# Left products of a depthwise convolution on GpSimd instead of VectorE, with a new order of pieces

## The chip, the cores and the metric

The kernel runs on one core of a Trainium2 chip. Its time is the device time of one execution in microseconds (us). Below, PE is TensorE (PEld its weight loads), DVE is VectorE, ACT is ScalarE, POOL is GpSimd and SP is SyncE.

## The reference

The program takes 32 samples of 128 tokens by 256 features, with a context of 128 by 192 each, through four layers. Each layer adds to x the output of a cross-attention and then of a feed-forward block, each times tanh of a gate. The four feed-forward blocks are a quantized pair of linear maps with a convolution between them, a mixture of experts with one expert per token, a small transformer block, and three blocks with dequantized weights. The change touches the first:

```python
h = bit_linear(x, w1)                                  # 256 -> 1024 features, quantized
h = depthwise_conv1d(h.transpose(0, 2, 1), conv_w, conv_b)   # 3 taps over the tokens, per channel
h = h.transpose(0, 2, 1)
h = jax.nn.silu(h)
return bit_linear(h, w2)                               # 1024 -> 256, quantized
```

A convolved value is its channel's left weight times the token before, plus the centre weight times the token itself, plus the right weight times the token after, plus a bias.

## The kernel before

Four lanes (0 to 3) each take one sample at a time, in eight passes, through two sequences of stages. The first is L0 (attention), bit (the block above), L1 (attention with wide heads) and route (the choice of experts); when all eight passes are through it, each lane goes on with mix, L2, self and L3, eight passes again. Eight lanes of a second kind then carry the last feed-forward block (L3f), four passes each. The sequence with the convolution ends near 1260 us; nothing in the second half has a convolution.

Every stage of every lane is written once per engine, as a generator that yields after each piece. An engine has one instruction queue, worked off in order. The order of the lanes' pieces in it is written out by hand or by a planner in the strings `ORDER` (L165): each character is the number of a lane, and `turns` (L331) runs that lane's generator to its next yield. So a piece waits not only for its semaphores but also for everything ahead of it in the string. Semaphores are counted by the names in `STAGE`, one counter for each lane and engine.

The stage bit, per lane and pass. VectorE normalizes and rounds x (L797 to L803); TensorE multiplies by w1 (h0 and h1, 512 columns of each of two PSUM banks). VectorE scales them into `hid`, 128 partitions by 8 channel groups by 128 tokens, in two halves of four groups (L809, signals hid0 and hid1). ScalarE makes the centre tap with the bias into `act_h` (L1288, four instructions for a half, signals cen0 and cen1). VectorE then adds the left products (L817, signal left) and the right products (L821, signal conv) to `act_h`. Each of these is a multiply-add with a weight per partition, so it takes one channel group of 127 tokens at a time, four instructions for a half, and L821 waits for L817's last. ScalarE makes tanh from it (L1295), VectorE the silu (L828), the maximum over the channels (L832) that TensorE transposes (L377), the scale (L836 to L840), the scaled and rounded values (L845, L851), which TensorE multiplies by w2 (L353), and the sum into x (L855).

GpSimd, before the change, does in the first sequence: variance and its power -1/2 for each normalization (`pool_rstd`, L1382 and L1384; VectorE's L711 waits for them), the keys of L0 spread over heads (L1399, two for a sample), bias sums (L1411, L1419), the softmax factors of L1 (L1424, four for a sample; TensorE's transposes L377 wait for them), the weight of the expert (L1442, L1444) and indirect DMAs (L1476, L1485, L1498). In the stage bit it has only `pool_rstd`.

`head_keys` are two buffers of 128 by 512 per lane, used by the attention stages L0 and L1 and free in between, during bit. `hid` and `act_h` are parts of the lane's buffer `big`, and `w["conv"]` holds three weights for each channel side by side. In the profile's names all of these are `big`, `head_keys` and `w_conv`.

Of the kernel before, what the change touches and what calls it, by code (L numbers as in the profile page):

```python
# [15 lines left out]
P = 128  # L16
# [44 lines left out]
        "pool": NORM["pool"],  # L61
# [94 lines left out]
def sequence_a(n):  # L156

    for half in (FIRST, SECOND):
# [8 lines left out]
        "3231314231212111323213121121213234230231023113100222200033331111313121323210301301030101131030200123"  # L167
        "2332131310210232021213212130120313012120323132013130120123121032302011312103302232332023020120122333"
        "3001220221001101312312132100101100210230203110210312300020231212231320130121033012201321302110132123"
        "1210323021011213032020320330232122301320320103313202132032031010023331213010201111200312302032013012"  # L170
        "3131322221002003131231213130323120132012031130231231210231302323131012021023003030223202332321301030"
        "1322022133033101010002121010201313113200120203012310130232120203001213223123131032013203112102303110"
        "2123102131202023031101122002303302321223013203012033132021302320311000233312130012011112003123020320"
        "1301201231232312211223331300202012331231310102202330211302121302210313213102320321102112023020203303"
        "1222100230313031313120301301201303330212010102121200113023012300301021301003201323232121201302310130"
        "2130210210331210120231121321012012013210321131132200230302223212301203023123012230120213310310103330"
        "3033202311321002330233210201101020103203011300220021323232130203210131012212103013023132321132132012"
        "1321210123123203012111032202032030230231313010033022322103303101031033002102110012303313100102012023"
        "0231320100201232312023012103210310130321320211213303210123012031021031232302102131312301220202103213"
        "2310033032112221331201313020323200101121220302123233032012213031013021121323131231321321121323321312"  # L180
        "3021000202113130203201312100101330120310123323030020132311121303223213120103230203211210010331312003"
        "2231213032031122013033323012020121323102123100012122133230023110310310210321032012312130100010230010"
        "2232311312323202300211021033103121203310213203203230212021010130220313202113212030302112131330010103"
        "3203103123223032030110220120112312333010212023120001210221303210130101213312030230032302121230031021"
        "2312001022032011201232011031231021312302320123111022102330310101330322323002301321210031013102302022"
        "3213013021201332301232032320212110003212333003011023103201310233131201303213002032313100322102130032"
        "2021013201202331121303100123120332301322131132103022020121130203203111001030130102321212033210303203"
        "2132001022122031023332103201223203031100123331132313021001013230213300102212130022021012302130233112"
        "1303100213120332301322131132103022020121130203230111313300101033203103123232021010322033323001220233"
        "2130202003310120230132231130230300102321123001012310010220302303122312123012302301123310232312310232"  # L190
        "1213020121203202323010111033130202223032013131202303211011221231023023121303212200102331003010201330"
        "1301322132132010032230211012213201023210213003101302030213221010033130222330113123120312032102302330"
        "3101110331302022230320131312320302101122121021302331312301133212030102133210301302301130102103213212"
        "133012201002083722870020283838702802370830a97879a80330738a979a0793a09738a30937a830a378a9a8b909cb87ca"
        "07b08acb8c8bc90b97ac0a8b78bc89ab789ab7a0c80a9c8b0ba9ca798a79bab8c7007ac8a0b870b87b0c8cb0a9a79769565c"
        "9cb6c5b65b6c59a65b9c7ac675ca675c659756b9ab5c658c96898598b5b966caca56a565ba56cb96cb79cb5c6956a756b9c7"
        "56c8bc97a5bc65b7687a9ca5c56677886c96596565bc5b98a96a56856a8b657b5789a6b956c5b7cb7c8b6ac685a578ac7a6c"
        "765865b659c7959b9b6cb6587a56c865c59ba796b565"
    ),
    "dve": (  # L200
        "1302130424413214213411441213221321323022131131313133132131212232321321301322203103030000100130120020"
        "2101301023013112123233033010232212231210113112102301101313132302032302120101310223323221231213232032"
        "3213201101002002002130103100320101010302102020132230231202112011331321033131121013001213212102012032"
        "0022032322312311203323231323023313013323120020013010132300110100203021200300133202222312331131303102"
        "0111302113120120210231213131032203023300202212311202333232132303331011200220030013132100011010203020"
        "2010030133222221020331103112011331311210130012131212010220302203203232212311203233231323023313013323"
        "1202000001010123311322210030000010202023023230120023133013301201311211012322121101200132212120213202"
        "0311300332031231320123330122333301320130210002033001001201301310302001122300122212200310223113111021"
        "1331311210331020112332112220003212100232002213213213203232302321333330310301200132023300002000331010"
        "1201021323113002221322122313023101101211331031211331302120102312100130222002232100213321302312202333"  # L210
        "3330313021032100233030000200110101003201311322130220102233220132111231330302013323002023201203001213"
        "0313213013112112123202201000200003212231321311331320303313021202312201130110201300033323100032120223"
        "2102131113323310131100020311202123202221232031300133220101311030231323301230212023011002211300231003"
        "3200133201232202131201031100332033011112301120212320122200300122101132230323113032103201032300221033"
        "1122101002310032031320332231221030121031100102113132302323021230212003002202103131130312333023133021"
        "0232021020031101210030323130321202321021013100102130313213103122232012220030012002032031313310121330"
# [1188 lines left out]
def pool_cross(pool, m, t, p, l, src):  # L1405
# [635 lines left out]
```

## Time and profile before

| | us |
|---|---|
| median of 3 runs | 2839.97 |
| lowest and highest | 2837.9, 2842.7 |
| the profiled execution | 2830.95 |
| its span, first to last instruction | 2829.7 |
| TensorE busy | 2597.7 (92%) |
| VectorE busy | 2187.3 (77%) |
| ScalarE busy | 1684.6 (60%) |
| GpSimd busy | 1134.9 (40%) |
| mean granted TensorE clock | 0.975 |

Busy time is a sum over the whole span. What a change to one stage is worth has to be read in that stage, so the views below take the stretch from 70 to 1250 us, in which the setup is over and the convolution's sequence runs, apart from the rest. In a row of the groups, "L817 DVE ... big<-big,w_conv ... x250 | 74.9, 361 | 10.1 <-ACT big L1288 10.0" is: line 817 on VectorE, what it writes and reads, 250 instructions, 74.9 us busy together, 361 ns the mean of one, and 10.1 us in which the engine stood idle before them, 10.0 of them ended by ScalarE's L1288. Instructions of one engine overlap a little, so busy time is less than count times mean.

### The profile page before, as it was taken

The page shows a single profiled execution, that of the slowest core. Times are in us where ns is not written, and L with a number is a line of the kernel's source. Part 1 is how long each engine was busy: PE and PEld are TensorE (multiplying, and loading weights), DVE is VectorE, ACT ScalarE, POOL GpSimd, SP SyncE. Part 2 cuts the span into 40 slices and gives each one's busy share as a digit, 9 for nine tenths or more (in the row PEclk, how much of TensorE's full clock was granted, in tenths as well). Part 3 has the DMA queues.
Part 4 walks back from the last instruction along what each step waited for, and adds up shares of the span by engine and source line. Part 5 has one row for each costly group of instructions (what it writes and reads, how often), then busy time and mean ns, then how long its engine had stood idle before and what let it go on. Part 6 is the DMA issues. An engine that isn't in the chain of part 4 may idle for free.

```text
span 2829.7 us, 60900 instructions
## 1 busy us (share of the span) xinstructions
PE 2597.7 (92%) x23748; PEld 2122.2 (75%) x23748; DVE 2187.3 (77%) x4794; ACT 1684.6 (60%) x4539; POOL 1134.9 (40%) x1981
## 2 busy tenths in 40 slices
PE   7797989899888989999899999999999999999999
PEld 5676767677666767777777777888787878788777
DVE  7868697877678587786767777787878787778998
ACT  4565666666555666666555555655656565656544
POOL 2132323323443543324454444333333333435676
PEclk9898999999899999999999999999999999999999
DMA  6000000000011121100012121100000000000110
GB/s 189 3 24 9 18 13 18 14 13 18 11 48 40 63 77 42 30 16 24 11 46 62 55 76 58 33 19 20 21 16 21 16 24 13 24 3 25 33 36 21
DMA packets 84168, 92.15 MB, mean 33 GB/s; under 512 B 15332, under 2 KB 77288, under 8 KB 83880
## 3 DMA queue, kind: packets, MB, share of 16 engines
q1 hardware_dynamic: 75432, 59.91, 6.9%
q0 software_dynamic: 8448, 28.34, 3.4%
q8 instruction: 188, 3.08, 0.5%
q14 instruction: 100, 0.82, 0.1%
HBM read 65.36 MB, written 22.85 MB: 31 GB/s over the span
## 4 chain that ended last, share of the span: by engine, by line
PE 63%; DVE 23%; ACT 5%; POOL 4%; issue 3%; DMA 1%; SPq 1%; DVEq 0%; POOLq 0%; ACTq 0%
PE psum L353 14%; PE psum L377 12%; PE psum L346 12%; PE psum L403 6%; DVE tiny L730 4%; PE psum L415 3%; PE psum L532 3%; DVE big L738 3%; PE psum L370 3%; PE psum L360 3%; PE psum L367 2%; PE psum L526 2%; PE psum L513 2%; DVE xn L711 1%; DVE tiny L766 1%
## 5 line engine op out<-in xcount | busy, mean ns | idle before, releaser
L377 PE MATMUL psum<-ident,big 128*128 128x128 f32 x2784 | 428.2, 285 | 66.2 <-ACT big L1219 22.4
L377 PEld LDWEIGHTS psum<-ident,big 128*128 128x128 f32 x2784 | 324.0, 145 | 140.2 <-ACT big L1219 49.3
L1219 ACT ACTIVATE big<-big 128x512 f32<-128x512 f32 x512 | 312.1, 631 | 170.4 <-DVE big L738 168.5
L730 DVE TENSOR_REDUCE tiny<-psum 128x8 f32<-128x1024 f32 x256 | 312.3, 1220 | 47.5 <-PE psum L403 42.8
L738 DVE TENSOR_TENSOR big<-psum,tiny 128x512 f32<-128x512 f32 x512 | 329.6, 685 | 8.8
L1382 POOL TENSOR_SCALAR tiny<-mv 128x1 f32<-128x1 f32 x224 | 53.0, 236 | 677.1 <-DVE mv L701 674.9
L403 PE MATMUL psum<-head_keys,small 64*128 64x256 f32 x2048 | 285.9, 403 | 19.7 <-ACT big L1226 10.9
L1399 POOL TENSOR_TENSOR head_keys<-big,head_rows 128x512 f32<-128x512 f32 x256 | 266.6, 1060 | 0.0
L1424 POOL TENSOR_TENSOR big<-big,tiny 128x512 f32<-128x512 f32 x128 | 133.8, 1052 | 308.2 <-DVE tiny L773 308.0
L403 PEld LDWEIGHTS psum<-head_keys,small 64*128 64x128 f32 x2048 | 185.3, 189 | 74.6 <-issue 56.9
L1263 ACT ACTIVATE big<-psum,tiny 128x128 f32<-128x128 f32 x512 | 181.7, 382 | 38.1 <-DVE tiny L768 37.6
L1226 ACT ACTIVATE head_keys<-psum 128x512 f32<-128x512 f32 x256 | 144.4, 599 | 39.9 <-PE psum L377 38.5
L377 PE MATMUL psum<-ident,small 128*128 128x128 f32 x896 | 154.6, 282 | 10.6 <-ACT small L1230 5.7
L711 DVE TENSOR_SCALAR xn<-x,mv,tiny 128x256 f32<-128x256 f32 x192 | 112.7, 588 | 64.9 <-POOL tiny L1384 64.5
L1226 ACT ACTIVATE big<-psum 128x512 f32<-128x512 f32 x256 | 146.0, 597 | 27.5 <-PE psum L377 25.4
L1384 POOL TENSOR_TENSOR tiny<-tiny,minus_half 128x1 f32<-128x1 f32 x224 | 129.1, 576 | 18.6
L377 PEld LDWEIGHTS psum<-ident,small 128*128 128x128 f32 x896 | 102.6, 141 | 43.0 <-issue 12.0
L346 PE MATMUL psum<-xnT,w_L 128*128 128x128 f32 x1024 | 127.3, 278 | 1.7 <-ACT xnT L1250 1.6
L346 PE MATMUL psum<-xnT,w_up 128*128 128x128 f32 x1024 | 126.0, 277 | 0.0
L532 PE MATMUL psum<-w_L,head_keys 128*128 128x256 f32 x512 | 124.7, 387 | 1.2 <-ACT head_keys L1273 1.1
L346 PEld LDWEIGHTS psum<-xnT,w_L 128*128 128x128 f32 x1024 | 120.3, 192 | 7.4 <-issue 3.4
L346 PEld LDWEIGHTS psum<-xnT,w_up 128*128 128x128 f32 x1024 | 119.2, 192 | 3.4 <-issue 2.5
(334 smaller groups left out, 6616.7 us busy)
## 6 DMA issues: line engine op xcount, KB each, us to landing
ctxT<-in_ctxT SPq DMA_DIRECT2D x64, 128.0 KB, 2.2
after_L_xattn<-x SPq DMA_DIRECT2D x64, 128.0 KB, 1.7
mixture_out<-spare SPq DMA_DIRECT2D x46, 128.0 KB, 1.7
x_in<-in_x SPq DMA_DIRECT2D x32, 128.0 KB, 2.2
mixture_in<-xn SPq DMA_DIRECT2D x32, 128.0 KB, 1.7
x_in<-after_L_xattn SPq DMA_DIRECT2D x32, 128.0 KB, 2.1
w_bits<-after_L_xattn SPq DMA_DIRECT2D x32, 128.0 KB, 2.1
spare<-in_L_w SPq DMA_DIRECT2D x2, 1024.0 KB, 7.2
```

What stands on the lines that cost most here:

```text
L346: last = pe.matmul(bank[:, j * S:(j + 1) * S], wt[:, k, n * P:(n + 1) * P], src[:, k, :], start=k == 0, stop=k == KD - 1)
L353: last = pe.matmul(bank[:, 0:n], srcT[:, k, :], wt[:, k, c0:c0 + n], start=k == 0, stop=k == chunks - 1)
L377: last = pe.transpose(bank[:, k * P:(k + 1) * P], src[:, k * P:(k + 1) * P], identity)
L403: last = pe.matmul(t.ab[:, half, cols], t.qT[rows, r, :], keys[rows, cols], start=True, stop=True)
L532: last = pe.matmul(t.b[:, 0:D], t.kT_wide[:, k, :], m.w["L1o"][:, CH * r + k, :], start=k == 0, stop=k == CH - 1)
L711: dve.tensor_scalar(dst, src, t.mv[:, 0:1], t.tiny[:, 1:2], ALU.subtract, ALU.mult).then_inc(*t.dve.tell(p, f"{l}.{out}{sub}"))
L730: dve.tensor_reduce(top, s8, AX.X, ALU.max).then_inc(*t.dve.tell(p, f"{l}.top{r}"))
L738: dve.tensor_tensor(t.e[half], s8[:, mine, :], top[:, mine].rearrange("p (h o) -> p h o", o=1).to_broadcast([P, CH, S]), ALU.subtract).the ...
L1219: last = act.activation(flat, flat, ACT.Exp, scale=DH ** -0.5)
L1226: act.activation(t.eTs[c].rearrange("p h s -> p (h s)"), t.ab[:, c % 2, :], ACT.Copy).then_inc(*t.act.tell(p, f"{l}.eT{c}"))
L1263: last = act.activation(t.e[half][:, j, :], t.ab[:, half, j * S:(j + 1) * S], ACT.Exp, scale=WIDE ** -0.5, bias=t.tiny[:, 8 + h:9 + h], ac ...
L1399: pool.tensor_tensor(t.head_keys[r], t.kT[:, r:r + 1, :].to_broadcast([P, CH, S]), m.head_rows[:].rearrange("p (h o) -> p h o", o=1).to_br ...
```

## The change

Three things. GpSimd gets a new function `pool_conv`, run in the stage bit after `pool_rstd`: for each half it waits for VectorE's hid of that half and multiplies the half's 4 groups of 127 tokens by the left weights in one instruction, into one of the two `head_keys` buffers; its signals are lp0 and lp1. VectorE, for each half, waits for the centre tap as before and also for the product, and adds the product to `act_h` in one instruction in place of four multiply-adds. The right products stay as they are. And the strings of all five queues are new: TensorE's, VectorE's, ScalarE's and SyncE's hold the same turns of each lane in another order, GpSimd's has 1308 turns where it had 1244.

```diff
@@ -58,7 +58,7 @@
         "act": "xiT rows cen0 cen1 th0 th1",
-        "pool": NORM["pool"],
+        "pool": NORM["pool"] + " lp0 lp1",
     },
@@ -164,117 +164,118 @@
 ORDER = {
     "pe": (
-        "3231314231212111323213121121213234230231023113100222200033331111313121323210301301030101131030200123"
...
+        "4312311423231203303220121033123203201320213210010101333030222232323200301103113232232130310333021320"
...
@@ -813,10 +814,9 @@
     for half in range(2):
         ks = range(4 * half, 4 * half + 4)
         dve.wait_ge(*t.act.at(p, f"{l}.cen{half}"))
-        for k in ks:
-            last = dve.scalar_tensor_tensor(t.act_h[:, k, 1:S], t.hid[:, k, 0:S - 1], m.w["conv"][:, k, 0:1],
-                                            t.act_h[:, k, 1:S], ALU.mult, ALU.add)
-        then(last, f"left{half}")
+        dve.wait_ge(*t.pool.at(p, f"{l}.lp{half}"))
+        then(dve.tensor_tensor(t.act_h[:, ks[0]:ks[-1] + 1, 1:S], t.act_h[:, ks[0]:ks[-1] + 1, 1:S],
+                               t.head_keys[half][:, :, 0:S - 1], ALU.add), f"left{half}")
@@ -1412,6 +1412,17 @@
+def pool_conv(pool, m, t, p, l):
+
+    for half in range(2):
+        sl = slice(4 * half, 4 * half + 4)
+        pool.wait_ge(*t.dve.at(p, f"{l}.hid{half}"))
+        pool.tensor_tensor(t.head_keys[half][:, :, 0:S - 1], t.hid[:, sl, 0:S - 1],
+                           m.w["conv"][:, sl, 0:1].to_broadcast([P, 4, S - 1]), ALU.mult
+                           ).then_inc(*t.pool.tell(p, f"{l}.lp{half}"))
+        yield
+
@@ -1522,6 +1533,7 @@
         yield from pool_rstd(pool, m, t, p, "bit")
+        yield from pool_conv(pool, m, t, p, "bit")
```

## Rows read from the trace of the kernel before

**Rows 1.** The page, its span and busy time of each engine (share, instructions).

```profile
span 2829.7 us, 60900 instructions
...
PE 2597.7 (92%) x23748; PEld 2122.2 (75%) x23748; DVE 2187.3 (77%) x4794; ACT 1684.6 (60%) x4539; POOL 1134.9 (40%) x1981
```

**Rows 2.** Windows, before and after 1250 us: columns as in the first line.

```profile
core 0: us, PE busy (x) PEld busy (x) DVE busy (x) ACT busy (x) POOL busy (x), PEclk, DMA share, GB/s
70.00:1250.00 1180.00, 1045.05 (x10380) 844.58 (x10379) 900.65 (x2304) 740.53 (x2256) 407.91 (x611) 0.95 0.09 27
1250.00:2830.00 1580.00, 1502.95 (x12988) 1241.12 (x12987) 1237.43 (x2396) 912.75 (x2214) 707.36 (x1307) 0.99 0.10 30
```

**Rows 3.** Waits of TensorE, 70 to 1250 us: total us, times, longest us.

```profile
PE psum L377 <- POOL big L1424: 20.0, 22, 3.1
PE psum L377 <- DVE big L832: 19.5, 11, 4.8
PE psum L377 <- DVE small L801: 13.3, 12, 3.3
...
PE psum L353 <- DVE small L851: 9.0, 8, 4.0
```

**Rows 4.** Chain of waits, pieces of L817: start us, us, what; first and last.

```profile
70.03 1.05 DVE big L817 x4
...
1039.95 1.05 DVE big L817 x4
```

**Rows 5.** Groups by line and shape, 70 to 1250 us: busy us, mean ns | idle before.

```profile
L817 DVE SCALAR_TENSOR_TENSOR big<-big,w_conv 128x127 f32<-128x127 f32 x250 | 74.9, 361 | 10.1 <-ACT big L1288 10.0
...
L711 DVE TENSOR_SCALAR xn<-x,mv,tiny 128x256 f32<-128x256 f32 x88 | 46.9, 533 | 36.7 <-POOL tiny L1384 36.4
L828 DVE SCALAR_TENSOR_TENSOR big<-big 128x512 f32<-128x512 f32 x62 | 45.3, 737 | 3.5 <-ACT big L1295 3.2
```

**Rows 6.** Single lines, whole run: duration ns least/median/most, first and last start.

```profile
L817 DVE SCALAR_TENSOR_TENSOR big<-big,w_conv x256: 317/344/1129, 69.9 to 1252.9; 128x127 f32<-128x127 f32 x128
...
L828 DVE SCALAR_TENSOR_TENSOR big<-big x64: 657/683/1554, 76.3 to 1255.3; 128x512 f32<-128x512 f32 x64
...
L809 DVE TENSOR_TENSOR big<-psum,xnT x64: 655/680/692, 61.6 to 1248.1; 128x512 f32<-128x512 f32 x64
...
L711 DVE TENSOR_SCALAR xn<-x,mv,tiny x192: 340/410/2554, 55.7 to 2613.1; 128x256 f32<-128x256 f32 x192
...
L1424 POOL TENSOR_TENSOR big<-big,tiny x128: 1028/1039/1991, 107.3 to 1326.8; 128x512 f32<-128x512 f32 x128
```

**Rows 7.** Timeline of VectorE at 238 us: start us, us, instructions.

```profile
237.96 1.10 DVE L817 SCALAR_TENSOR_TENSOR big<-big,w_conv 128x127 f32<-128x127 f32 x4
239.10 1.14 DVE L821 SCALAR_TENSOR_TENSOR big<-big,w_conv 128x127 f32<-128x127 f32 x4
```

**Rows 8.** Timeline of VectorE, ScalarE and GpSimd from 240 to 244 us.

```profile
240.29 2.21 POOL L1399 TENSOR_TENSOR head_keys<-big,head_rows 128x512 f32<-128x512 f32 x2
...
240.47 1.13 DVE L711 TENSOR_SCALAR xn<-x_in,mv,tiny 128x256 f32<-128x256 f32 x1
...
241.52 1.27 DVE L809 TENSOR_TENSOR big<-psum,xnT 128x512 f32<-128x512 f32 x2
...
242.24 1.65 ACT L1288 ACTIVATE big<-big,w_convb,w_conv 128x128 f32<-128x128 f32 x4 [1.29 <-DVE big L809]
...
242.46 0.72 POOL L1419 TENSOR_TENSOR x<-x,out_bias_L 128x256 f32<-128x256 f32 x1
...
243.15 0.77 POOL L1411 TENSOR_TENSOR x<-x_in,out_bias_L 128x256 f32<-128x256 f32 x1
```

**Rows 9.** Windows in slices of 147 to 148 us, columns as in rows 2.

```profile
660.00:807.00 147.00, 122.75 (x1171) 98.63 (x1170) 111.80 (x287) 86.08 (x259) 54.30 (x75) 0.91 0.06 17
807.00:955.00 148.00, 135.34 (x1338) 109.77 (x1339) 113.62 (x302) 95.48 (x294) 63.13 (x92) 0.98 0.16 51
...
1400.00:1547.00 147.00, 133.76 (x1192) 108.77 (x1192) 106.25 (x186) 79.05 (x189) 80.68 (x125) 0.99 0.16 48
...
1842.00:1990.00 148.00, 143.71 (x1329) 120.23 (x1328) 114.64 (x193) 87.75 (x212) 57.90 (x110) 1.00 0.07 20
```

More of the change, by code:

```diff
@@ L172 @@
[L172 to L176, printed above, removed]
@@ new lines @@
+        "2132313231022023313311022121021303212013130212302231103100031313020120131213003031102011023222332312"
+        "0031002122132312103103230321033120131133130323031220133203302201200021201321322003201232103213103202"
+        "2210130110031230320311031210013103020101231031232313212300201032232323102310313012303202130310313210"
+        "1303123320200202023102231233001031202123021203201101020212323103010330030310132102020311323123121231"
+        "3312132113222221200001311202123302301321230320131203132303211120323033201022120203023112023123021230"
@@ new lines @@
+        "2231031313011232103203110130311030131001301213130023110110232020200331200010232132323232032013310130"
+        "1322310213032301302310213212133033012102120203100321203123123200312312012312123121012222331013010330"
+        "3031013210121012301203120321131012020320303003031231202002012332132101233103103213023012020313032312"
+        "0212110210223123030221010120122021321021231301032201221010330113010303013120123001210312002011201103"
+        "2303322123103000123222102103130123022301231012032112313003032132321002202033322131202132123303000123"
@@ new lines @@
+        "3122203023102323210101232023321130021023111002131203103020301231311312333113231232211312213213122120"
+        "1202020302133130012033232300313013221032010232301013313201120332131202133123130310321223230203322120"
+        "0311012320320320132013021013102122130310320332100111313022311321002302301201301230120131232121213023"
+        "0200203212002033130023130201301301321001022011321333012123121023130210230212013103131300320232200103"
+        "2033011013220201101301220121201321230303023223010233111010320110310323023112312310210010230312213230"
@@ new lines @@
+        "0122021233300213032030130132132012012020321333011221230110013031032120123321002132310313101030330121"
+        "0321022311213103212013230210203323201133212100303112312320030211031031031012332132112320310202020313"
+        "2200310312121020201123010320213132030102120213313022133201232013032013000123132001020230110213102213"
+        "0210302323232002203131132002103130232011301003211312132123013002310112202133322100203321310230132030"
+        "1020121201032313131321202013313221201233123231303001103133200222101213010021201020322312312121231300"
@@ new lines @@
+        "3021312131102131121023232331302010302000130002111322132021303312033012010103133120221232202312202300"
+        "30b0cb01c20c1bc1b2bc1011bcbc0b2c1bcbc209a9a11b1babcac09cab90b19abca090cb9ba9c01ba9ac90cbb0090aca9ab9"
+        "bca9ca91b09cbacb9c1a97ba87c89a7cb87a8cba97089a7ba78a9897c9a8c7a087b8acb09658569875897567856a8756785a"
+        "96865789ca6b57657869cba56567586a758657b68958697c565876957986a587568796a58567568a75687c5a67c865a78c67"
+        "5c85868765c7ab675bc686b5c8a6a5c568596ac957c5976a65cab769b5a96b5896785b7968b95875689675786b7"
```

175 lines of the change are left out of this document (78 added, 97 removed).

## The prediction

> **What bounds the kernel now.** I read the page first: TensorE is busy 2597.7 of 2829.7 us, VectorE 2187.3, ScalarE 1684.6, GpSimd 1134.9 [rows 1]. So TensorE carries the time, but not evenly. The windows view split at 1250 us, where the stages with the convolution end, shows it [rows 2]: from 70 to 1250 us TensorE is busy 1045 of 1180 us (88.6%, 135 us idle), afterwards 1503 of 1580 us (95.1%, 77 us idle). In the first stretch VectorE is busy 901 us (76%) and GpSimd 408 us (35%). At the second stretch's rate the first would have 58 us of idle TensorE, so about 77 us is the room that better-fed matmuls could ever give there. The granted clock is also lower, 0.95 against 0.99 [rows 2].
>
> Then I read what TensorE waits for in the first stretch [rows 3]. At the head stand GpSimd's products L1424 (20.0 us), the channel maximum L832 (19.5 us), the rounding L801 (13.3 us) and L851 (9.0 us). L832 and L851 come behind the convolution on VectorE, in one lane's serial chain; L801 is in the same stage, ahead of it. So the convolution does reach TensorE, in small portions. The chain of waits says how often. Of the 64 groups of left products (L817, four instructions each) 22 lie on the chain that ended last; most take 1.03 to 1.06 us, a few are stretched; all 22 together 26.6 us (the first and the last stand in [rows 4]).
>
> **The change part by part.** *Removed:* 256 instructions at L817, median 344 ns [rows 6]. They overlap in VectorE's pipe, so counts times means would overstate them. A group starts at 237.96, and the next group, L821, which waits for it, starts at 239.10: 1.14 us for four [rows 7], 0.04 us of it the gap after the 1.10 us. *Added on VectorE:* one add over 128 x 508 with both inputs in SBUF. No row has exactly this. The nearest are L809 (128x512, one input in PSUM, median 680 ns) and L828 (128x512, all in SBUF, median 683 ns) [rows 6]. I take 0.68 plus the gap of 0.04: 0.72 us. The bounds are 0.65 (the least of L828 is 657 ns) and 0.74 us, since L828's mean with its collisions is 737 [rows 5, 6]. Saved: 0.42 us for a group, 64 x 0.42 = 27 us of VectorE; the bounds of the add make that 26 to 31.
>
> What of it lies on the path: 22 groups x 0.42 = 9.2 us, and a little of the stretched ones. That is the term: -10 us. Its upper bound is the whole 27 us, if every group were on the path in the new order; its lower bound 0, if what is late next stands right behind each. The other 42 groups lie beside other work and give nothing by themselves.
>
> *Added on GpSimd:* 64 multiplications of 128x508. The nearest row is L1424, the same kind with a broadcast factor over 128x512: 1039 ns median [rows 6]. 64 x 1.04 = 67 us, which takes GpSimd from 408 to 475 us of 1180 (40%). Cover: the add waits for the product and for ScalarE's centre tap. After hid0 (L809, from 241.52, two in 1.27 us, so the first ends at 242.20) ScalarE starts four L1288 at 242.24 and the fourth ends 1.65 us later [rows 8]. The product needs 1.04 us from the same moment, so it is hidden by 0.6 us if GpSimd is free. For the second half ScalarE is 1.65 us further, GpSimd 1.04 us: hidden more deeply. If GpSimd is not free the cover goes. In the same picture GpSimd is busy without a break from 240.29 to 243.92 [rows 8], and a product asked for at 242.20 would come 1.7 us plus 1.04 us later, 1.1 us behind the centre tap. GpSimd is busy a third of the time, mostly with one instruction of 1 us, so I count one group in ten as late by 1 us: 6 us, of which VectorE's chain share below makes 2 us. Bounds: 0, and 64 x 1.1 us x 0.34 = 24 us.
>
> *The new wait's queue.* GpSimd works in a fixed order. Behind a product that waits for hid0 or hid1 stand the other lanes' variance and power steps (L1382, L1384), for which VectorE's L711 waited 36.4 us already [rows 5], and the L1424 products. In the new order both products of a sample stand next to each other in most of the 32 passes, and hid1 comes one turn after hid0 in most, so this wait is mostly 0. Queueing: GpSimd is 6% more busy, a step that finds a product ahead of it waits half of 1.04 us, 0.03 us on average over the 611 instructions and DMA issues of the stretch [rows 2], 18 us in all, of which GpSimd's place on the path (L1424's 20 us of TensorE's waits [rows 3] against 128 instructions of 1.04 us [rows 6], one seventh) leaves 3 us. Bounds 0 and 9 (half of the 18).
>
> *Contention.* VectorE's instructions stretch where a GpSimd instruction runs. L817 took up to 1129 ns against 344, L711 up to 2554 against 410 [rows 6], and at 240.47 an L711 took 1.13 us beside L1399 [rows 8]. In the first stretch the means stand above the medians by 123 ns for 88 L711 on x, 17 ns for 250 L817 and 54 ns for 62 L828, together 18 us [rows 5, 6]. These are three forms of about ten that can be hit, so I take twice that, 36 to 40 us. Against GpSimd's 408 us it is 0.1 us of stretch for each us; as part of the 408 are DMA issues, which stretch nothing that I see, I take 0.12. 67 us more give 8 us of VectorE. What part reaches the end: L817 has 26.6 of its 74.9 us on the chain, 36% [rows 4, 5]. At 36% it is +3 us. Bounds: 0 (512 exposed instructions become 320), and 64 x 0.52 us = 33 us of stretch if every product holds up one instruction for half its length.
>
> The Trainium skill ("GPSIMD Engine Reference", Key points) has this contention for VectorE instructions in a two-port mode or with two SBUF inputs; the trace agrees, since L809 with an input in PSUM never exceeded 692 ns [rows 6]. The same page (Engine selection) speaks against the change: elementwise work belongs on VectorE, GpSimd being about 2x slower with two inputs. The rows give 1.04 against 0.68 us, 1.5x. By the page's factor the product would be an estimated 1.36 us, still under the centre tap, and the sum would be about 2 us worse.
>
> *Order of pieces.* All five orders are new: the same turns on four queues, and 1308 for 1244 on GpSimd. TensorE's turns count the same, and nothing is added or removed from 1250 us on. The order's luck has no row of its own. I bound it by how much equal work varies under one order: in eight slices of 147 to 148 us of the first stretch TensorE is idle between 12.7 and 24.3 us, in seven of the second between 4.3 and 13.2 (the least and the most of each: [rows 9]). With a deviation of some 4 us a slice in the first and 3 in the second, 8 and 10 slices give 4 x 2.8 = 11 and 3 x 3.2 = 10 us, together +-15 us as an outer size; slices of one order also vary by what falls into them, so I take +-10. An order laid out for a VectorE with a net 27 - 8 = 19 us less work, on a path with VectorE on a third of it, can use more than the groups now on the path: I give it a third of those 19 us less what is counted, rounded to -5 us, bounds +-10 around it.
>
> *Sum:* -10 + 2 + 3 + 3 - 5 = -7 us. The profiled span is 2829.7 us (2831 us with what lies around it), the median of the runs 2840.0, 9 us above it. I carry the difference over: 2822.7 us in a profile, 2833 us in the median.
>
> **The rivals.**
> *Hidden anyway.* TensorE is at 88.6 to 95.1%, and no row shows TensorE waiting for L817 or L821 themselves. The next wait, L1424 or L711, takes the place: 2839 us. For it: the small portions, 22 of 64. Against: L832's 19.5 us come straight after this chain.
>
> *GpSimd becomes the late one.* Place: between hid0/hid1 and the add, and every VectorE instruction that meets a product. Price: 33 us of stretch x 0.36 = 12 us instead of 3; late products 6 us instead of 2; queue 6 instead of 3; against the 10 us of gain: 12 + 6 + 6 - 10 = +14 us less some of the order's gain, 2851 us. It decides from the point where more than about one product in two holds up a VectorE instruction on the path, or products start more than 0.6 us after hid. The page's two rules named above point this way.
>
> *The order fills TensorE.* If a third of the 77 us of room is found, -26 us: 2814 us. For it: 135 us idle in pieces of 1 to 3 us, and a lower clock (0.91 of the upper level of 2.4 GHz in the slice where TensorE is least busy [rows 9]) that could come back with denser matmuls. Against: dependence and the other engines' load hardly change.
>
> *It does not do what it says:* the three-float step between the channel weights slows the product beyond L1424's. It would have to exceed 1.65 us to show, and then joins the GpSimd case.
>
> **How the numbers follow.** Forecast 2833 us: 45%, own range 2826 to 2841. Hidden anyway: 18%. GpSimd late: 17%. Order fills TensorE: 20%. A measurement of this kernel can tell about 0.2%, 5.7 us (2834.3 to 2845.7), from no change. Faster than that: 29 points of the forecast, 19 of the order, 1 of hidden, 49%. Same: 14 + 13 + 2 + 1 = 30%. Slower: 2 + 4 + 15 = 21%. The range takes the order's centre with a little below and GpSimd late with a little above: 2812 to 2853 us, leaving out some 10% on each side.
>
> **What would show it.** After: the add at the place of L817, 64 instructions with a median near 0.68 us; the new GpSimd line, 64 at 1.04 us; VectorE about 19 us less busy before 1250 us; VectorE's waits for the new line a few us in all (over 10 us: GpSimd late); TensorE's waits for L832 down by some us and for L1424 not up by more than 5. The stretch before 1250 us should shorten by about 7 us and the rest stay within 5 us. If the rest moves more, or the first stretch moves by more than 12 us, the order did it, not the convolution.

## The result and the profile after

| | us |
|---|---|
| kernel after, median of 4 runs | 2869.35 (2868.75 to 2869.84) |
| kernel before, beside it, median of 4 | 2839.15 (2837.9 to 2842.7) |
| ratio, 95% interval | 1.0108 [1.0096, 1.0119] |
| spans of the profiled executions, before and after | 2829.7 and 2867.5 |

The change makes the kernel 1.1% slower, 30 us, where 7 us faster was forecast, and 16 us beyond the upper end of the range. The profiled execution of before was 8 us quicker than its median, and that of after 0.6 us, so the difference of the two spans, 37.8 us, holds some 8 us that are not the change's.

The page of the kernel after, its busy times and the shares of the chain that ended last:

```profile
PE 2608.6 (91%) x23748; PEld 2125.9 (74%) x23748; DVE 2182.6 (76%) x4602; ACT 1691.5 (59%) x4541; POOL 1226.4 (43%) x2045
...
PE 62%; DVE 22%; POOL 6%; ACT 6%; issue 3%; DMA 1%; SPq 1%; another core or an unknown queue 0%; DVEq 0%; POOLq 0%; ACTq 0%
```

Against [rows 1] GpSimd is 91.5 us busier, VectorE only 4.7 us less busy (27 us were to be taken off it), and TensorE is busy 11 us longer with the same 23748 matmuls, and idle 27 us more. The windows before and after 1250 us, columns as in [rows 2]:

```profile
70.00:1250.00 1180.00, 1037.31 (x10249) 839.83 (x10248) 883.22 (x2094) 726.99 (x2209) 478.65 (x668) 0.95 0.08 27
1250.00:2868.00 1618.00, 1529.84 (x13195) 1254.57 (x13195) 1254.90 (x2445) 939.43 (x2276) 724.41 (x1320) 0.99 0.10 29
```

In the same 1180 us TensorE gets through 131 matmuls fewer than before [rows 2]. The new and the old lines of the convolution (duration ns least/median/most, first and last start), and who waits for the product:

```profile
L818 DVE TENSOR_TENSOR big<-big,head_keys x64: 648/678/1518, 84.3 to 1281.0; 128x508 f32<-128x508 f32 x64
...
L821 DVE SCALAR_TENSOR_TENSOR big<-big,w_conv x256: 336/346/1127, 85.2 to 1282.4; 128x127 f32<-128x127 f32 x128
...
L1420 POOL TENSOR_TENSOR head_keys<-big,w_conv x64: 1033/1041/1484, 81.6 to 1276.5; 128x508 f32<-128x508 f32 x64
its engine sat idle before it (us, times) until:
  DVE big L810: 82.5, 22
who waited for it (us, times):
  DVE big L818: 4.3, 2
```

Both prices were right to a few ns: 678 for the add, 1041 for the product. The product is waited for twice, 4.3 us. Yet everything comes late: the first convolution starts at 84 us, where before's starts at 69.9 [rows 6], and the last L821 at 1282.4, where before's starts at 1254.1. So 14 us are lost before the first instruction that the changed computation touches, and 14 more up to the end of the convolution's stages. From there to the end the kernel after takes 1585.1 us and before 1575.6. These 9.5 us are about what the two executions differ by anyway: in the runs further down on chips where the kernel before took 2832 us this last part is 1573.9 to 1577.1 us, with either of the two orders, and on those where it took 2839 to 2841 us 1584.8 to 1589.4. The 14 us at the start are seen in TensorE's waits of the first 70 us (line waited for: us, times, longest), of before:

```profile
PE psum L635 <- DVE bvb L1023: 9.6, 1, 9.6
PE psum L377 <- ACT big L1219: 4.5, 6, 1.8
PE psum L641 <- DVE absum L1064: 2.5, 1, 2.5
```

and of after (L642 is before's L641, L636 is L635, and L637 makes the output bias of L1):

```profile
PE psum L642 <- DVE absum L1064: 11.0, 1, 11.0
PE psum L636 <- DVE bvb L1023: 9.8, 1, 9.8
PE psum L637 <- DVE w_L1bo L1020: 6.5, 1, 6.5
```

Two setup turns of TensorE (the character 4) stand early in the new strings. TensorE's first turn there is the mean of the weights' absolute values (L642), and its eighth the product with L1's output bias (L637). Both need loaded weights that VectorE has treated. In before they are turns 7 and 34, and other lanes' matmuls run meanwhile. In the timeline of the kernel after, TensorE's first projection (L361) stands behind the mean, at 24.4 us; in before the same one (L360) is at 13.3:

```profile
24.00 0.56 PE L642 MATMUL psum<-absum,ones 128*128 128x2 f32 x2 [11.01 <-DVE absum L1064]
24.42 1.20 PE L361 MATMUL psum<-ctxT,w_L0k 128*128 128x128 f32 x4
```

```profile
13.31 1.22 PE L360 MATMUL psum<-ctxT,w_L0k 128*128 128x128 f32 x4 [0.52 <-DVE out_bias_L L1029]
```

What TensorE waits for from 70 to 1290 us in the kernel after (L1435 is [rows 3]'s L1424, L802 its L801, L712 its L711):

```profile
PE psum L378 <- POOL big L1435: 28.3, 25, 6.2
PE psum L378 <- DVE big L832: 27.1, 10, 15.4
PE psum L378 <- DVE xn L712: 15.9, 15, 2.3
PE psum L378 <- DVE small L802: 10.2, 7, 5.5
```

L832 was to fall and L1424 was not to rise by more than 5; they rose by 7.6 and 8.3 us. One wait of 15.4 us for L832, near 97 us, holds more than that rise. The rise at L1424 is not the product's either: in the new order without any product (the first experiment below) TensorE waits 27.7 us for it.

### The profile page after: what moved, and what is told of

Its sections match the earlier page's. It is cut to its first block, busy times and chain, and to the rows that moved or that the text cites. A ratio compares the mean times of both kernels' runs of the same rounds, so it can differ in the third digit from the quotient of the medians.

```text
span 2867.5 us, 60841 instructions
## 1 busy us (share of the span) xinstructions
PE 2608.6 (91%) x23748; PEld 2125.9 (74%) x23748; DVE 2182.6 (76%) x4602; ACT 1691.5 (59%) x4541; POOL 1226.4 (43%) x2045
## 4 chain that ended last, share of the span: by engine, by line
PE 62%; DVE 22%; POOL 6%; ACT 6%; issue 3%; DMA 1%; SPq 1%; another core or an unknown queue 0%; DVEq 0%; POOLq 0%; ACTq 0%
PE psum L354 14%; PE psum L378 13%; PE psum L347 10%; PE psum L404 6%; PE psum L416 4%; DVE tiny L731 3%; PE psum L371 3%; PE psum L533 3%; PE psum L361 3%; DVE big L739 3%; PE psum L368 2%; PE psum L527 2%; DVE big L821 2%; PE psum L514 1%; DVE xn L712 1%
## 5 line engine op out<-in xcount | busy, mean ns | idle before, releaser
L378 PE MATMUL psum<-ident,big 128*128 128x128 f32 x2784 | 422.8, 283 | 86.2 <-POOL big L1435 28.3
L1435 POOL TENSOR_TENSOR big<-big,tiny 128x512 f32<-128x512 f32 x128 | 138.7, 1089 | 259.1 <-DVE tiny L774 258.7
L712 DVE TENSOR_SCALAR xn<-x,mv,tiny 128x256 f32<-128x256 f32 x192 | 107.0, 560 | 59.2 <-POOL tiny L1384 58.4
L1384 POOL TENSOR_TENSOR tiny<-tiny,minus_half 128x1 f32<-128x1 f32 x224 | 135.2, 603 | 18.7
L378 PEld LDWEIGHTS psum<-ident,small 128*128 128x128 f32 x896 | 103.4, 143 | 50.1 <-ACT small L1230 12.9
L1230 ACT ACTIVATE small<-psum 128x512 f32<-128x512 f32 x128 | 76.6, 599 | 91.2 <-PE psum L416 78.9
```

The source lines that it names most:

```text
L378: last = pe.transpose(bank[:, k * P:(k + 1) * P], src[:, k * P:(k + 1) * P], identity)
L1435: pool.tensor_tensor(t.e[c % 2], t.e[c % 2], rc.to_broadcast([P, CH, S]), ALU.mult).then_inc(*t.pool.tell(p, f"{l}.n{c}"))
```

## The experiments

Three things changed at once: the computation, the order's first turns and the order of the rest. Three theories: the order (its start, or the rest); the product's cost on GpSimd (late, in other pieces' way in its queue, occupying the engine, or colliding with VectorE); the saving hidden anyway. Ratios below are to the kernel before run on the same chip; 0.1% is 2.8 us.

### The order and the computation apart

The new order with the old computation. GpSimd's string is the new one without its 64 product turns:

```diff
-        dve.wait_ge(*t.pool.at(p, f"{l}.lp{half}"))
-        then(dve.tensor_tensor(t.act_h[:, ks[0]:ks[-1] + 1, 1:S], t.act_h[:, ks[0]:ks[-1] + 1, 1:S],
-                               t.head_keys[half][:, :, 0:S - 1], ALU.add), f"left{half}")
+        for k in ks:
+            last = dve.scalar_tensor_tensor(t.act_h[:, k, 1:S], t.hid[:, k, 0:S - 1], m.w["conv"][:, k, 0:1],
+                                            t.act_h[:, k, 1:S], ALU.mult, ALU.add)
+        then(last, f"left{half}")
...
-        yield from pool_conv(pool, m, t, p, "bit")
```

> The new order of all five queues with the old computation: VectorE makes the left products with four multiply-adds again, GpSimd has no product (its two turns a pass are taken out of its string, nothing else). Theory A, the order makes the kernel slower (its start is about 13 us late, and more is lost up to 850 us): 2860 to 2875 us, since only the product, worth a few us either way, is missing. Theory B, the product on GpSimd makes it slower (queue, lateness, contention): 2835 to 2850 us.

2858.41 us against 2832.22: 1.0093 [1.0076, 1.0110]. The order alone costs 26 us. It also changes what VectorE's left products are worth. The chain that ended last, up to 1290 us, by line, as shares of these 1290 us (the view ends where the line does):

```profile
by line: PE psum L377 9.6%; PE psum L346 7.7%; DVE big L817 5.2%; PE psum L353 5.0%; PE psum L532 5.0%; DVE big L821 4.7%; PE psum L370 3.8%; PE psum L403 3.7%; PE psum L360 3.5%; PE psum L526 3.3%; issue 3.2%; PE psum L367 3.1%; DVE big L8
```

L817 has 5.2% of it, 67 us, in 55 of the 64 groups; in before it had 26.6 us in 23 groups (the prediction counted 22). L821 went from 30 to 61 us.

The new computation with the old order. The five strings are before's; the 64 product turns are set into GpSimd's where hid0 or hid1 was ready in the trace of before.

> The old order of TensorE, VectorE, ScalarE and SyncE with the product on GpSimd and the one add on VectorE; GpSimd's old string with a product turn put in where its input was ready in the profile of before. Theory A: 2825 to 2840 us, as forecast for the mechanism without the order's part (-2 us, with -10 of gain, +8 of costs). Theory B: 2855 to 2870 us.

2832.74 us: 1.0001 [0.9991, 1.0011]. The computation alone is worth nothing and costs nothing, within 3 us. Its product is never waited for; these are its rows:

```profile
L1420 POOL TENSOR_TENSOR head_keys<-big,w_conv x64: 1027/1039/1487, 62.9 to 1252.4; 128x508 f32<-128x508 f32 x64
its engine sat idle before it (us, times) until:
  DVE big L810: 78.8, 28
who waited for it (us, times):
```

### The product taken down to one token, in both orders

```diff
-        pool.tensor_tensor(t.head_keys[half][:, :, 0:S - 1], t.hid[:, sl, 0:S - 1],
-                           m.w["conv"][:, sl, 0:1].to_broadcast([P, 4, S - 1]), ALU.mult
+        pool.tensor_tensor(t.head_keys[half][:, :, 0:1], t.hid[:, sl, 0:1],
+                           m.w["conv"][:, sl, 0:1], ALU.mult
```

The left products of the other 126 tokens are left out. The kernel after with this edit:

> The changed kernel, but the product on GpSimd is made for 1 of the 127 tokens, so its left taps are wrong; the instruction, its wait and its signal stay, its 1.05 us shrinks to some 0.2. Theory A: 2860 to 2870 us, GpSimd's 54 us less of work give back up to 8 us. Theory B (time of the product and its contention): 2840 to 2850 us.

2836.55 us: 1.0008 [0.9999, 1.0018], lower than either theory had it. The old order with it:

> As the kernel with the old order and the product on GpSimd, but the product made for 1 of 127 tokens (left taps wrong). By the forecast's sum the costs of the full product are 3 us of contention, 3 of queueing and 2 of lateness, so this is 5 to 8 us below the kernel with the full product. Theory B: 15 to 25 us below it.

2826.32 us: 0.9989 [0.9977, 1.0000]. Taking four multiply-adds for one add gives 3 us in the old order and 24 in the new (1.0093 to 1.0008). The product's length takes back 3 us in the old and 28 in the new (1.0008 to 1.0108). These go by the ratios; by the medians both 3 us are 6, and the 24 us are 22. The 24 us agree with the chain of the new order: 55 groups of 0.42 us are 23. The busy times on the pages of the four, in this order: after, after with one token, old order with the product, old order with one token:

```profile
PE 2608.6 (91%) x23748; PEld 2125.9 (74%) x23748; DVE 2182.6 (76%) x4602; ACT 1691.5 (59%) x4541; POOL 1226.4 (43%) x2045
```

```profile
PE 2599.8 (92%) x23748; PEld 2123.5 (75%) x23748; DVE 2165.1 (76%) x4602; ACT 1687.4 (60%) x4541; POOL 1168.1 (41%) x2045
```

```profile
PE 2595.6 (92%) x23748; PEld 2121.6 (75%) x23748; DVE 2175.8 (77%) x4602; ACT 1682.2 (59%) x4539; POOL 1207.3 (43%) x2045
```

```profile
PE 2601.5 (92%) x23748; PEld 2124.5 (75%) x23748; DVE 2162.9 (77%) x4602; ACT 1683.3 (60%) x4539; POOL 1155.5 (41%) x2045
```

VectorE loses 17.5 us to the full-size products in the new order (2182.6 less 2165.1) and 12.9 in the old. The collisions cost VectorE something of the same size in both; what the product costs the kernel, 28 us against 3 to 6, differs several times over. The kernel after with one token also starts late: its hundredth matmul ends 16.0 us behind before's, as in the kernel after (16.2). It ends 2 us behind all the same.

### Which part of the product's cost it is

Late, or not: the one-token product signals at once, and behind it GpSimd does a full-size multiplication of constants into a buffer that nothing reads.

```diff
+        m.behinds += 1
+        pool.tensor_tensor(m.behind[:].rearrange("p (k s) -> p k s", k=4),
+                           m.causal[:, 0:S - 1].rearrange("p (o s) -> p o s", o=1).to_broadcast([P, 4, S - 1]),
+                           m.w["conv"][:, sl, 0:1].to_broadcast([P, 4, S - 1]), ALU.mult).then_inc(m.behind_sem, 1)
```

> The changed kernel; the product is made for 1 of 127 tokens and signals at once, and behind it GpSimd makes a product of the full size from constants into a buffer that nobody reads (the left taps are wrong). So VectorE never waits for the full product, but GpSimd is as busy as in the changed kernel and collides with VectorE as often. If lateness of the product is what costs: about 2840 us, near the kernel with the small product alone (1.001 of before). If GpSimd's busy time costs, by collisions with VectorE and by the steps queued behind it: 1.008 to 1.011 of before, 2855 to 2865 us.

2869.87 us against 2840.51: 1.0100 [1.0083, 1.0117], the kernel after again. The add has its product early and nothing is gained. GpSimd is 9 us busier than in the kernel after (1235.3 against 1226.4), and the intervals leave room for a gain of some 8 us, but not for the 28: with waits of 4.3 us in all, lateness is at most a small part.

In the way of other pieces, or not: 13 of the 64 product turns moved by one or two places in GpSimd's string, behind or ahead of another lane's piece, to where the trace of after has their input ready.

```diff
-        "3201333111222000323320123232010133220101330302332333121222220031013300001011211122332023300212113300"
+        "3201333111222000323322013232001133220101330302332333121222220031013300001011211122332023300212113300"
```

> The changed kernel with the product's turns set elsewhere in GpSimd's order, where their input stood ready in the profile of the new order without products (13 of 64 moved, by one or two turns, nothing else changed). If other lanes' steps queued behind products that wait for VectorE's hid cost much: at least 8 us below the changed kernel, 2855 us or less. If GpSimd's busy time itself costs: within 4 us of the changed kernel, 1.010 of before.

2870.97 us: 1.0104 [1.0088, 1.0121]. No gain: moving these 13 is worth nothing beyond the interval. An order with the products far from where they are was not tried.

Occupying or colliding: the one-token product, and behind it two powers of one column, so that GpSimd is at least as busy but its added work is not wide.

```diff
+        for cell in range(2):
...
+            pool.tensor_tensor(m.behind[:, cell:cell + 1], m.ones[:, 0:1], m.minus_half[:],
+                               ALU.pow).then_inc(m.behind_sem, 1)
```

> The kernel after, in which the product is made for one of the 127 tokens alone and signals at once, and two operations on one number for each partition (a power, some 0.57 us each by the rows of L1384) follow it on GpSimd. So GpSimd's order and its busy time are those of the kernel after, but no wide GpSimd instruction lies beside VectorE's. If GpSimd's time costs the 28 us because its other work (the products L1435, the signs and masks) comes later, the ratio to the kernel before stays at 1.009 to 1.011. If it costs them by the collisions (an instruction of VectorE is stretched to the end of a wide one of GpSimd), the ratio falls to that of the kernel with the short product, 1.001 to 1.003. In between, both are at work, in the proportion in which it lies.

2861.74 us against 2838.85: 1.0074 [1.0057, 1.0091]. Its new line and its page:

```profile
L1427 POOL TENSOR_TENSOR behind<-ones,minus_half x128: 539/550/882, 81.0 to 1268.5; 128x1 f32<-128x1 f32 x128
...
PE 2601.4 (91%) x23748; PEld 2122.0 (74%) x23748; DVE 2169.3 (76%) x4602; ACT 1690.0 (59%) x4541; POOL 1237.8 (43%) x2173
```

VectorE is busy 2169 us, near the one-token kernel's 2165 and 13 us below the kernel after. So 128 powers, 0.55 us each by the median, hardly touch VectorE. Of the product's 28 us in this order some 19 (1.0008 to 1.0074) are GpSimd's time as such. That is rather too much than too little, since GpSimd is 11 us busier here than in the kernel after. The remaining 10 (1.0074 to 1.0108) go with the wide instruction. The two intervals, [1.0057, 1.0091] and [1.0096, 1.0119], lie close together, so that the split is rough. By which pieces the 19 us reach TensorE is not shown: it waits for L1435 26.9 us with one token, 28.3 in the kernel after and 30.0 here, and VectorE for the powers L1384 33.8, 34.8 and 33.2, all of which is too little.

### The order's start

The kernel before with nine setup turns (TensorE's two, VectorE's first seven) at the places of the new strings. The first characters of TensorE's and of VectorE's string:

```diff
-        "3231314231212111323213121121213234230231023113100222200033331111313121323210301301030101131030200123"
+        "4323131423121211132321312112121323230231023113100222200033331111313121323210301301030101131030200123"
-        "1302130424413214213411441213221321323022131131313133132131212232321321301322203103030000100130120020"
+        "1344021340244441321213111213221321323022131131313133132131212232321321301322203103030000100130120020"
```

> The kernel before, with nothing changed but the places of nine setup turns: the two turns of TensorE and the seven first ones of VectorE that prepare constants stand where the order made anew has them (TensorE's first turn waits for the mean of the weights, and with it for a 2 MB load). The theory that the new order's loss is in its start: the first softmax comes 10 to 15 us later and nothing gives it back, ratio 1.004 to 1.005. The rival, that a late start is regained because other waits shrink: 0.999 to 1.001.

2858.55 us against 2838.85: 1.0062 [1.0045, 1.0078], 18 us. TensorE's waits in its first 70 us are those of the kernel after:

```profile
PE psum L641 <- DVE absum L1064: 11.3, 1, 11.3
PE psum L635 <- DVE bvb L1023: 9.6, 1, 9.6
PE psum L636 <- DVE w_L1bo L1020: 8.8, 1, 8.8
```

The hundredth matmul ends 18.1 us later than in before, the thousandth 17.8, the eight thousandth 20.5: in the old order a late start is carried to the end. Here nine of some 10,000 turns cost 18 us, two thirds of what the whole new order costs. That this is also their share in the new order does not follow: the kernel after with one token starts 16 us late too and regains nearly all of it.

Then the reverse: the kernel after, its turns of the first 60 us among themselves in the old order.

```diff
-        "4312311423231203303220121033123203201320213210010101333030222232323200301103113232232130310333021320"
+        "3231314231212111323232223234303000001320213210010101333030222232323200301103113232232130310333021320"
```

> The kernel after, in which the turns that its order has in about the first 60 us (25 of TensorE's, 20 of VectorE's, 25 of ScalarE's, 5 of GpSimd's change place) stand in the old order among themselves; every later turn stays. The setup turns that TensorE waits for are then as late as in the kernel before. If the late start is a cost of its own that everything later only passes on, the loss of the kernel after falls by that start's 13 to 16 us: ratio 1.004 to 1.007. If the new order's later turns are laid out for its own start (its fourth lane is begun 20 turns earlier than the old one's), the time gained is waited away at the seam, and the ratio stays at 1.009 to 1.012.

2857.29 us against 2831.62: 1.0088 [1.0071, 1.0105]. At the hundredth matmul it is 1.3 us ahead of before, at the three hundredth 18 us behind, at the thousandth 21.6. Its waits of the first 70 us, and from 70 to 120 us:

```profile
PE psum L378 <- ACT big L1219: 10.2, 4, 4.5
PE psum L636 <- DVE bvb L1023: 9.8, 1, 9.8
PE psum L642 <- DVE absum L1064: 1.5, 1, 1.5
...
PE psum L378 <- DVE big L832: 16.7, 2, 15.4
```

The setup waits are gone and others have come at the seam: the later turns are laid out for other places of the lanes (the fourth one begins with TensorE's 15th turn, before's with the 37th). The wait of 15.4 us for L832 is the same with either start. VectorE's timeline in the kernel after shows what it is:

```profile
89.68 0.68 DVE L818 TENSOR_TENSOR big<-big,head_keys 128x508 f32<-128x508 f32 x1
90.39 1.14 DVE L821 SCALAR_TENSOR_TENSOR big<-big,w_conv 128x127 f32<-128x127 f32 x4
91.45 0.68 DVE L828 SCALAR_TENSOR_TENSOR big<-big 128x512 f32<-128x512 f32 x1
92.05 0.68 DVE L818 TENSOR_TENSOR big<-big,head_keys 128x508 f32<-128x508 f32 x1
92.77 1.14 DVE L821 SCALAR_TENSOR_TENSOR big<-big,w_conv 128x127 f32<-128x127 f32 x4
93.82 1.89 DVE L828 SCALAR_TENSOR_TENSOR big<-big 128x512 f32<-128x512 f32 x3
95.62 3.65 DVE L832 TENSOR_REDUCE big<-big 128x128 f32<-128x1024 f32 x2
```

Two samples' four halves go through the convolution side by side, from 84 to 94 us, and both maxima follow, while TensorE waits for the first of them. In before the six halves of three lanes start at 70, 74, 80, 84, 89 and 94 us, each lane's maximum soon after its second (79, 92, 99 us), so that TensorE gets work in between. So the loss can't be mended by these first turns alone: 1.0108 became 1.0088, with intervals that overlap.

### Other orders of the same work

A list planner of our own, with durations from the traces, searched new strings for the new computation (from the old order, and from the order of after) and for the old computation. Nothing but the five strings differs: the first and the third kernel below have the source of the kernel after, the second that of before. TensorE's string of the first, against before's:

```diff
-        "3231314231212111323213121121213234230231023113100222200033331111313121323210301301030101131030200123"
+        "2313231213124111222333111122112332430230121301301222020033331113131100321232113030130101320300012132"
```

> The computation of the kernel after (the product on GpSimd, one add on VectorE) with a third order of pieces. It was searched from the old order with a list planner of our own, which takes each instruction's duration from the traces, knows the waits, lengthens a two-input VectorE instruction to the end of a wide GpSimd one beside it, and keeps an order that is good also when durations are a few per cent off. If the slowdown of the kernel after is its order and not its computation, another order of the same computation is at least as fast as the kernel before: ratio 0.985 to 1.000. If the computation costs by itself (GpSimd's time and the collisions), no order of it comes below 1.000, and this one, unlike the two that were planned with more care, lands at 1.005 to 1.02.

> The computation of the kernel before (four multiply-adds on VectorE), its order searched in the same way and for as long. Beside mech_new it gives the price of the computation with orders of one make. Saving 27 us of VectorE is worth something: this kernel is slower than mech_new by 3 to 12 us (0.1 to 0.4%). The product's own costs on GpSimd eat all of it: within 3 us of it or faster. Against the kernel before it can be anything from 0.985 to 1.01.

> The same source as mech_new, but the search set out from the order of the kernel after in place of the old one. If that order's loss can be repaired by local moves of pieces, it comes to the kernel before or below it, 0.990 to 1.003. If the loss is in its large pattern (how the samples of the four lanes are staggered against each other), it stays 0.5 to 1% behind mech_new.

2885.09, 2895.49 and 2923.24 us against 2832.32: 1.0182 [1.0165, 1.0199], 1.0216 [1.0199, 1.0233] and 1.0309 [1.0287, 1.0330]. None comes near the two given orders. The first lies where it was expected if the computation costs by itself, but the second, with the old computation, is slower still, so the searched orders are poor with either computation. The second and the third missed the ranges given against the kernel before. An order of the new computation that beats before was not found, and it is not shown that there is none. The first two differ by 10 us, inside what was expected of the computation, but with orders that scatter like this the 10 us prove nothing. TensorE's part on the page of the first:

```profile
PE 2635.3 (91%) x23748; PEld 2131.6 (74%) x23748; DVE 2168.9 (75%) x4602; ACT 1692.7 (59%) x4537; POOL 1204.5 (42%) x2045
```

The same matmuls keep TensorE busy 38 us longer than in [rows 1], against 16 us of more idle time (2883.7 less 2635.3, to 2829.7 less 2597.7). An order moves busy time too, which a plan made of fixed durations does not see. The clock is a small part of it: the mean granted clock is 0.972 against 0.975, which by our estimate is at most 9 of the 38 us (0.003 of 2884). The rest was not pursued.

## Why the prediction was wrong

**The step that failed is the order's term,** "-5 us, bounds +-10 around it". It measured +26 us. Its size was taken from how much slices of one order vary, which says how unevenly a good order works and nothing about how far another order may lie from it: five orders stand in this text, and the four that are not before's cost +26, +52, +61 and +88 us with one computation or the other. Its sign was taken from a lighter VectorE. That effect exists, and is larger than thought: the lighter VectorE is worth 24 us in the new order and 3 in the old. But it was priced against an order that costs nothing by itself. And a part of the cost could be read in the diff. The step said "TensorE's turns count the same" and did not read where they stand. The string of the new TensorE queue begins with a setup turn whose input VectorE has not before 24 us in the profile of before (L641 starts at 24.46), where TensorE works from 13.3 us on: 11 us that way, and 6.5 more at L637. The start alone, put into the old order, costs 18; the old start, put into the new order, gives back some 6, so that most of the 26 us can't be assigned to single turns.

**The saved VectorE time,** "22 groups x 0.42 = 9.2 us". The sizes held: VectorE is 24.4 us less busy with a one-token product in the old order (2187.3 less 2162.9), for 27 forecast. What reaches the end in the old order is 3 us with its interval from 0 to 6.5, not 9 or 10. In the new order it is 24, where the same count on that order's chain gives 23 (55 x 0.42). So the count was too high for the order that it was read from, and came out, by this one comparison, for the order that it stood for, whose chain it was not read from. The rival "hidden anyway" was right in the number for the computation alone (1.0001), but half by luck: a small saving and an equally small cost of the product cancel.

**Lateness and queue,** +2 and +3. The product is waited for 4.3 us in all after, never in the old order, and both experiments on them moved nothing beyond their intervals. Small, as said. (The bound of 24 us for late products takes a share of 0.34 where the text derives 36%; it would be 25.)

**Contention,** 8 us of VectorE and +3 at the end. VectorE lost 17.5 us (12.9 in the old order), twice the forecast: an L818 beside GpSimd took up to 1518 ns, where its median is 678. 0.12 us for each us of GpSimd was an average over all its 408 us, of which only 184 are in pieces of 128x512 like the product, and 117 in one-column pieces, the kind that hardly touches VectorE. In the old order the end still moved by only 3 us (6 by the medians), for contention and occupation together. In the new one it moved by 28. Of these some 10 go with the width; the term was sized by the old order's chain (36%), and 36% of 17.5 would be 6.

**What GpSimd's time as such costs** had no term but the queueing of 3 us. In the new order it measured about 19, and by which path is open.

**The rival that came nearest** is "GpSimd becomes the late one", 2851 us. It priced the product's costs at 24 us (12 + 6 + 6), and in the new order they measured 28. But it set 10 us of gain against them and came to +14, where the gain was 24 and the net 4 (1.0093 to 1.0108). Its conditions were wrong too: the products start on time and the wait at the add is small. That its time lies nearest to 2869 is luck: the missing 26 us are the order's.

**The signs named beforehand** told it right: "if the first stretch moves by more than 12 us, the order did it". It moved by 28 us (last L821 from 1254.1 to 1282.4), in the kernel with the order alone too (1282.0), and in the old order with the product by 2.5 us (last L821 at 1256.6). The rest was to stay within 5 us and is 9.5 longer, which the section on the result puts down to the executions. VectorE was to be 19 us less busy before 1250 us and is 17.4, with less of the work done by then.

**Open.** That the saving weighs 24 us in one order and 3 in the other fits the two chains, 55 groups of left products against 23, but what puts them there no run isolates. The reading that fits is that the new order, which takes two lanes side by side through a stage as at 84 us, has one lane's next step directly behind another's on VectorE, where the old one has slack. Why the same product on GpSimd costs 28 us in one order and 3 to 6 in the other is not settled; what is shown is that it does.

## What to carry to other kernels

Time a new static order with the old computation, and the new computation in the old order, before judging either: here the +30 us were an order that costs 26 by itself and a computation worth 0 in the old order and 4 more in the new one. Read the first turns of each queue in the diff against the times at which their inputs were ready in the trace; a setup turn that waits at the head of the bottleneck engine cost 18 us here where the engines behind it were loaded as before, though with the one-token product a start 16 us late was nearly all regained. What a saving or a cost on another engine is worth depends on the order, so a price read from one order's chain is not a price in another.

## What the runs showed of the hardware

One column of GpSimd work and 508 columns of it are different neighbours for VectorE. 128 powers on 128x1 (70 us by their median) left VectorE's busy time at 4.2 us above that of the kernel without them; 67 us of products on 128x508 added 12.9 to 17.5 us to it, both against the one-token product. (The powers are also another operation than the products; width and operation were not taken apart.) The Trainium skill ("GPSIMD Engine Reference", Key points) names the conflict for VectorE's instructions with two SBUF inputs or a two-port mode; the traces agree in kind, and the busy times above give it a size here, 0.19 to 0.26 us of VectorE for each us of the wide multiplication.

The same 23748 matmuls kept TensorE busy 2595.6 us (old order with the product) to 2641.4 us (the last of the searched orders), with the same source except for the order. A part of it is the clock: around a pause of TensorE of 4.5 us that ends at 1433.3 us, the kernel after has a granted clock of 0.67 on the mean from 1430 to 1440 us, a mixture of the levels of 2.4 and 1.2 GHz, and 0.89 from 1420 to 1480 us (the column ahead of the last two). In the slice from 1400 to 1547 us it has 0.95, where before has 0.99 [rows 9]:

```profile
1420.00:1480.00 60.00, 48.10 (x378) 37.59 (x375) 34.61 (x61) 27.27 (x62) 34.37 (x49) 0.89 0.10 28
```
